# Layer 1 of a two-layer graph network: three product slices folded on GpSimd, thirteen summed on TensorE, extras and additions interleaved

## The reference, cut to what matters

```
R = relu(abs_distances[:, None] @ w1 + b1) @ w2 + b2      # 384 radial weights per edge
Y = spherical_harmonics(rel_vec)
Fj = features[src]                                         # 8 scalars, 8 vectors of 3
for each output block i (lo), input block j (li), lf:
    acc = acc + _NORM[i] * einsum('euv,ef,evi,ofi->euo', Rb[..., k], Yf, Fb, C)
out = zeros.at[dst].add(msg)
x = layernorm(x + out)
```

## Time and profile before

| | us |
|---|---|
| median of 3 runs (lowest to highest) | 1683.98 (1680.54 to 1688.54) |
| the profiled execution's own time | 1679.48 |
| its span | 1677.5 |
| TensorE busy (matmul) | 1287.4, 77% |
| VectorE busy | 1219.6, 73% |
| GpSimd busy | 1007.6, 60% |
| ScalarE busy | 837.2, 50% |
| mean granted TensorE clock | 0.855 |

### The profile page before, as it was taken

One profiled execution on the slowest core, in us unless ns is written; L12 is line 12 of the kernel. 1 busy time (PEld: TensorE's weight loads), 2 busy tenths in 40 slices (PEclk: granted clock), 3 DMA queues, 4 the chain that ended last, 5 costly groups with the idle time before them and its releaser, 6 DMA issues.

```text
span 1677.5 us, 26088 instructions
## 1 busy us (share of the span) xinstructions
PE 1287.4 (77%) x6396; PEld 930.4 (55%) x6396; DVE 1219.6 (73%) x3753; ACT 837.2 (50%) x2256; POOL 1007.6 (60%) x1084
## 2 busy tenths in 40 slices
PE   5699994686413777665677999975999999995773
PEld 1388883243212555555565666653777777775663
DVE  9699996677622343576667999983888888883776
ACT  0167771011101222566675777763665666554984
POOL 7777778777777777776111344446888666600444
PEclk8699997586755999988888999996999999997655
DMA  1100001223224889666455566631232223213785
GB/s 39 23 14 14 15 14 23 51 68 77 69 66 120 250 244 252 173 173 172 119 136 137 172 181 190 184 106 45 61 75 63 59 59 70 65 40 84 204 216 154
DMA packets 310023, 179.32 MB, mean 107 GB/s; under 512 B 29294, under 2 KB 303346, under 8 KB 309874
## 3 DMA queue, kind: packets, MB, share of 16 engines
q1 hardware_dynamic: 231234, 116.84, 26.7%
q0 software_dynamic: 29008, 36.18, 8.6%
q10 hardware_dynamic: 49632, 24.65, 5.1%
HBM read 111.48 MB, written 66.07 MB: 106 GB/s over the span
## 4 chain that ended last, share of the span: by engine, by line
PE 39%; POOL 25%; issue 15%; DMA 10%; DVE 6%; DVEq 2%; ACT 2%; SPq 1%; POOLq 0%; ACTq 0%
PE bank L1042 13%; POOL gat L536 12%; PE bank L1008 7%; POOL lined L544 7%; DMA lined<-in_x,other_i 5%; DVE res L1351 4%; PE bank L1035 3%; DMA placed<-pay,pos_i 3%; PE bank L959 3%; PE bank L1051 3%; POOL out L603 3%; PE bank L1001 3%; PE bank L1017 3%; PE bank L961 2%; POOL placed L555 2%
## 5 line engine op out<-in xcount | busy, mean ns | idle before, releaser
L593 POOL DMA_INDIRECT gat<-x_d,src_i x196 | 238.2, 1215 | 94.8 <-issue 55.7
L1351 DVE TENSOR_TENSOR res<-res,bank 128x128 f32 x588 | 168.5, 287 | 107.2 <-issue 22.6
L536 POOL DMA_INDIRECT gat<-in_x,key_i x196 | 207.0, 1056 | 61.9 <-issue 55.5
L555 POOL DMA_INDIRECT placed<-pay,pos_i x196 | 191.6, 978 | 69.8 <-issue 53.9
L544 POOL DMA_INDIRECT lined<-in_x,other_i x196 | 196.1, 1000 | 59.9 <-issue 48.6
L1042 PE MATMUL bank<-prod,ident 128*128 128x280 f32 x896 | 219.8, 404 | 0.0
L1042 PEld LDWEIGHTS bank<-prod,ident 128*128 128x128 f32 x896 | 168.7, 191 | 54.1 <-issue 15.2
L970 PE MATMUL bank<-woh,pw 128*128 128x128 f32 x784 | 133.4, 332 | 71.4 <-DVE woh L1330 35.8
L970 PEld LDWEIGHTS bank<-woh,pw 128*128 128x128 f32 x784 | 118.5, 235 | 86.7 <-DVE woh L1330 46.2
L56 ACT ACTIVATE xt<-bank 128x128 f32<-128x128 f32 x98 | 26.6, 271 | 264.8 <-PE bank L910 256.2
L890 PE MATMUL bank<-tile_oh,sel 128*128 128x196 f32 x784 | 142.6, 336 | 2.9 <-ACT tile_oh L663 2.0
(11 more groups left out here) (221 smaller groups left out, 2886.2 us busy)
## 6 DMA issues: line engine op xcount, KB each, us to landing
pw<-placed SPq DMA_DIRECT2D x588, 68.0 KB, 2.1
pw<-placed SPq DMA_DIRECT2D x98, 272.0 KB
xin<-in_x_t SPq DMA_DIRECT2D x53, 256.0 KB
placed<-pay SPq DMA_DIRECT2D x49, 272.0 KB, 2.4
x_d<-res POOLq DMA_DIRECT2D x49, 256.0 KB, 3.8
placed<-pay SPq DMA_DIRECT2D x28, 448.0 KB, 3.2
out<-out ACTq DMA_DIRECT2D x49, 256.0 KB, 2.7
xin<-in_x_t ACTq DMA_DIRECT2D x45, 256.0 KB
```

The source lines that it names most:

```text
L536: pool.indirect_dma_start(gat[:, t, :], None, x, bass.IndirectOffsetOnAxis(ap=key_i[:, 0, t:t + 1], axis=0)).then_inc(s_gat[t % G], 16)
L555: pool.indirect_dma_start(placed[1].rearrange("t p r -> (t p) r"), bass.IndirectOffsetOnAxis(ap=pos_i[:, 1, t:t + 1], axis=0), pay[i % 4][ ...
L593: pool.indirect_dma_start(gat1[g % 3][:, k, :], None, x1_d, bass.IndirectOffsetOnAxis(ap=src_i[:, t:t + 1], axis=0)).then_inc(c_gat[g % 3] ...
L1351: add.up(dve.tensor_tensor(into, into, quarter(bank + k // G, k % G), ALU.add))
```

## The change

GpSimd's program gets a second kind of work: `fold_3(g)` adds slices 3 to 5 of `prod[g % 2]` onto slices 0 to 2, in place, when VectorE has written them. It is put behind `gather_3(g + 3)`. TensorE sums slices 6 to 15 first, then waits for the fold (`c_fold`), then sums slices 0 to 2: 13 matmuls. The extras now come one round later, between the second and the third pair of radial steps. On VectorE message and additions are one function: the register read comes first, then the wait for the extras, then message operations and additions in turn (four additions between message operations, three behind the payload). The arithmetic differs only in the order of additions.

```diff
@@ gpsimd
-            for g in range(NU):
-                gather_3(g)
+            def fold_3(g):
+                pool.wait_ge(c_prod, g + 1)
+                some = prod[g % 2][:, :, 0:FOLD, :].rearrange("p t v u -> p t (v u)")
+                more = prod[g % 2][:, :, FOLD:2 * FOLD, :].rearrange("p t v u -> p t (v u)")
+                pool.tensor_tensor(some, some, more, ALU.add).then_inc(c_fold, 1)
+
+            for g in range(NU + 3):
+                if g < NU:
+                    gather_3(g)
+                if g >= 3:
+                    fold_3(g - 3)
@@ tensor
-            def radial(g):
+            def radial(g, lo, hi):
                 pe.wait_ge(c_ht, g + 1)
-                for k in range(0, U, 2):
+                for k in range(lo, hi, 2):
...
-                for v in range(16):
+                for v in [*range(2 * FOLD, 16), *range(FOLD)]:
+                    if v == 0:
+                        pe.wait_ge(c_fold, g + 1)
...
-            radial(0)
-            for g in range(NU + 1):
+            radial(0, 0, U)
+            for g in range(NU + 2):
                 if g + 1 < NU:
-                    radial(g + 1)
+                    radial(g + 1, 0, PAIRED)
+                if g >= 2:
+                    extras(g - 2)
+                if g + 1 < NU:
+                    radial(g + 1, PAIRED, U)
                 if g < NU:
                     sums(g)
-                if g:
-                    extras(g - 1)
@@ vector
+            def message_and_extras_3(g):
+
+                h, behind = g % 2, 0 <= g - 1 < NU
+                to = windows_at(U * (g - 1), U, 1) if behind else None
+                if behind:
+                    dve.wait_ge(c_mm, g)
+
+                def extra(k):
+                    if behind:
+                        add_tile(5, k, to)
+
+                if g < NU:
+                    along = rec[:, U * g:U * g + U, 3:6].unsqueeze(2).broadcast_to([P, U, 8, 3])
+                    dve.wait_ge(c_scal, g + 1)
+                    chain.up(dve.tensor_tensor(rq[:, :, :, :], rest[:, :, 0:8].unsqueeze(3).broadcast_to([P, U, 8, 3]), along, ALU.mult))
+                extra(0)
...
+                extra(3)
+                if g < NU:
+                    dve.wait_ge(c_msg, g + 1)
+                    wait(dve, c_pst[h], 16 * (g // 2))
+                    wait(dve, c_mm, g - 1)
+                    dve.tensor_tensor(pay1[h][:, :, :].rearrange("p t (j f) -> p t j f", j=J),
...
+                for k in range(4, U):
+                    extra(k)
@@
-                if 1 <= g <= NU:
-                    message_3(g - 1)
-                if g >= 2:
-                    extras_3(g - 2)
+                if g:
+                    message_and_extras_3(g - 1)
```

More of the change, by code:

```diff
@@ L300, in gnn_kernel @@
         c_prod, c_sum, c_scal, c_pay, c_mm, c_msg = sem("c_prod"), sem("c_sum"), sem("c_scal"), sem("c_pay"), sem("c_mm"), sem("c_msg")
+        c_fold = sem("c_fold")
         z_pw, z_kr, z_away, z_oh, z_mm = ring(sem, "z_pw", 6), sem("z_kr"), sem("z_away"), sem("z_oh"), sem("z_mm")
@@ L428, in gnn_kernel @@
         RADIAL = (0, 1, 2, 7)
+        PAIRED = 4
+        FOLD = 3
         block = ctx.enter_context(nc.Block())
@@ L1040, in sums @@
                 wait(pe, c_scal, g - 1)
-                for v in range(16):
+                for v in [*range(2 * FOLD, 16), *range(FOLD)]:
+                    if v == 0:
+                        pe.wait_ge(c_fold, g + 1)
                     ins = pe.matmul(psum[3 + g % 2][:, 0:40 * U].rearrange("p (t u) -> p t u", t=U), ident[:, :], prod[g % 2][:, :, v, :],
-                                    start=v == 0, stop=v == 15)
+                                    start=v == 2 * FOLD, stop=v == FOLD - 1)
                 ins.then_inc(c_sum, 1)
@@ L1341, in _, with windows_at @@
             add = Count(s_add)
-            def add_tiles(bank, t0, n, c):
+            def windows_at(t0, n, c):
                 _, to = nc.values_load_multi_w_load_instructions(
@@ L1347, in add_tiles, with add_tile @@
                     skip_runtime_bounds_check_because=IN_RANGE)
+                return to
+            def add_tile(bank, k, to):
+                into = res[:, bass.ds(to[k], 1), :].rearrange("p o c -> p (o c)")
+                wait(dve, add.sem, add.n)
+                add.up(dve.tensor_tensor(into, into, quarter(bank + k // G, k % G), ALU.add))
+            def add_tiles(bank, t0, n, c):
+                to = windows_at(t0, n, c)
                 for k in range(n):
-                    into = res[:, bass.ds(to[k], 1), :].rearrange("p o c -> p (o c)")
-                    wait(dve, add.sem, add.n)
-                    add.up(dve.tensor_tensor(into, into, quarter(bank + k // G, k % G), ALU.add))
+                    add_tile(bank, k, to)
             def add_extra(i, c):
@@ L1454, in products_3 @@
                 ins.then_inc(c_prod, 1)
[L1456 to L1474, removed]
@@ L1476, in extras_3 @@
-            def extras_3(g):
-                dve.wait_ge(c_mm, g + 1)
-                add_tiles(5, U * g, U, 1)
+            def message_and_extras_3(g):
[12 more added lines that the diff above has]
+                if g < NU:
+                    done(chain)
+                    chain.up(dve.tensor_tensor(msg[:, :, 8:32].rearrange("p t (u i) -> p t u i", i=3), rq[:, :, :, :],
+                                               rest[:, :, 8:32].rearrange("p t (i u) -> p t u i", i=3), ALU.add))
+                extra(1)
+                if g < NU:
+                    done(chain)
+                    chain.up(dve.tensor_reduce(mean[:, :], msg[:, :, :], AX_X, ALU.add))
+                extra(2)
+                if g < NU:
+                    done(chain)
+                    dve.scalar_tensor_tensor(out=msgc[:, :, :], in0=mean[:, :].unsqueeze(2).broadcast_to([P, U, D]), scalar=-1.0 / D,
+                                             in1=msg[:, :, :], op0=ALU.mult, op1=ALU.add).then_inc(c_msg, 1)
+                extra(3)
+                if g < NU:
+                    dve.wait_ge(c_msg, g + 1)
+                    wait(dve, c_pst[h], 16 * (g // 2))
+                    wait(dve, c_mm, g - 1)
+                    dve.tensor_tensor(pay1[h][:, :, :].rearrange("p t (j f) -> p t j f", j=J),
+                                      msgc[:, :, :].unsqueeze(2).broadcast_to([P, U, J, D]),
+                                      jm[:, U * g:U * g + U, :].unsqueeze(3).broadcast_to([P, U, J, D]), ALU.mult).then_inc(c_pay, 1)
+                for k in range(4, U):
+                    extra(k)
```

## The result

| | before | after |
|---|---|---|
| median of the runs, us | 1682.6 (4 runs, 1680.5 to 1688.5) | 1702.1 (4 runs, 1693.5 to 1707.0) |
| ratio | | 1.0097 [1.0055, 1.0138] |
| the profiled execution: time (span), us | 1679.5 (1677.5) | 1693.5 (1691.6) |

The changed kernel is slower: the ratio gives 1.0%, and the two medians lie 19.5 us apart. (The four runs of before include the profiled one; their median is therefore not the 1684.0 of the prediction.) The profiled execution of the changed kernel is its shortest run, 14.1 us longer in span than that of before.

The account below looks back on a forecast made before the run. Took TensorE as the bound before and GpSimd's queue after: start +7.9, rounds +16.6, last three -1, tail -0.8, together +22.7 us on 1679.5, 1702.2; on the median 1706.7, stated as 1706, range 1674 to 1724.

Parts of the forecast that it names:

- the rounds: Layer 1 from sums(0) to sums(24): GpSimd sets 13.6 us a round, 24 x 13.6 = 326.4 against 309.8, +16.6 us.
- the start: Layer 1 up to the end of sums(0): the last three terms wait for gather(3) and the first fold, +7.9 us.
- the last three: Layer 1 rounds after sums(24), without gathers: VectorE sets them, about 34 us against 35.0, -1 us.
- TensorE's part: TensorE's round in Layer 1: three sum terms go, 1.45 us; round 10.6 to 11.5 us, taken as 11.4.
- The extras between radial pairs: TensorE's round: extras (1.56 us) fill waits for ScalarE's evictions inside the radial pairs; bounds nothing and 0.9 us.
- VectorE's part: VectorE's round with messages and additions alternated and an uncovered register read of 1.8 us: 11.9 us if nothing else happens.
- The fold: GpSimd's addition of 840 elements per partition: 2.0 us, during which a VectorE operation with two SBUF inputs stands still.
- Losses shrink: Rival: GpSimd's round locks so one gather meets products, 12.45 to 13.0 us; at 12.7, 1685 us; chance 0.17.
- the forecast (13.1 to 14.2): Main case: GpSimd's round in Layer 1 is 13.1 to 14.2 us, time 1694 to 1721 us; chance 0.57.
- the rival in which both engines pay: VectorE loses 2.0 us at each fold and waits for registers; round 14.2 to 14.5, 1723 us; chance 0.12.
- The tail: End of Layer 1 after the last sums: 6.1 us for the last extras and alternated run against 6.9, -0.8 us.
- the marks for the right side: Signs: folds about 2.0 us, sums(0) ending near 1180, sums 13.6 apart, TensorE waiting for GpSimd ahead of the last terms.

Follow-up runs that it names:

- experiment 1: The changed kernel without the fold: TensorE sums sixteen terms again, new order of extras, messages and additions kept; 1679.0 us, 0.9986 against the kernel before.
- experiment 5: The changed kernel with each fold replaced by a GpSimd memset of 1340 elements into an unread tile; 1663.8 us, 0.987 against the kernel before.
- experiment 2: The kernel before with the fold alone, 13 sums and no other part of the change; 1692.9 us, 1.009 against the kernel before.
- experiment 6: The changed kernel with fold(g) behind gather(g+2) and not gather(g+3); 1688.7 us, 1.0048 against the kernel before.
- experiment 3: The changed kernel with the window register read moved from ahead of the message to behind the first product; 1704.7 us, 1.0177 against the kernel before.
- experiment 4: The changed kernel with five gathers a group, not seven, from the fourth group on; 1683.0 us, 1.0031 against the kernel before.

## Why the prediction was right, and where its steps were not

The forecast, GpSimd's queue as the new bound and a slower kernel, came true: predicted 1706, range 1674 to 1724, measured 1702.1. The terms, on the profiled execution (predicted +22.7, measured +14.1), came out less well than the total, and that the total is so near is in part luck: the rounds were put 13.2 us too high, the start and the last three together 6.3 too low, and the unprofiled runs lie above the profiled one for a reason that stays open.

**TensorE's part: right, and worth nothing.** Three terms less is 1.4 us (7.81 to 6.40), and TensorE's own round is below the others'. The extras between radial pairs, which I bounded by 0 and 0.9 and gave 0.1, gave 0.02 in experiment 1.

**VectorE's part: right, 0.4 too long.** I had 11.9 without a block. Its round with a fill in the fold's place is 11.53, and the changed kernel's round less the block is 13.12 - 1.61 = 11.51. The register read costs 1.62 from fk to rq where I took 1.8, the alternated starts are 0.20 to 0.26 apart where I counted 0.21 to 0.31, and the run from rq to products is 3.95 (in experiment 5, where nothing stretches msgc) instead of 4.1.

**The fold: right.** 1.98 us against 2.0. That it stretches a VectorE operation with two SBUF inputs to its own length was right too, from one row: msgc 2.01, rq 1.99, kp 2.09.

**The start: right in kind, 7.9 for 10.0.** The last three terms took 3.17 and not 1.45, which is 1.7 of the 2.1 missing. The table of windows has those 3.17 us (length, busy us of PE, PEld, DVE, ACT, POOL, granted clock):

```profile
1177.29:1180.46 3.17, 3.17 (x8) 1.92 (x10) 0.00 (x0) 0.00 (x0) 2.45 (x3) 0.50 0.05 9
```

The clock is 0.50, the lower of the two levels (1.2 GHz of 2.4), behind 8.85 us in which TensorE did nothing. Of all terms this one has the firmest proof: experiment 2 has it without the new order (+10.2), experiment 6 takes it away by moving the fold.

**The rounds: the step that was mis-sized.** "I take 13.6" is 13.10, and "24 x 13.6 = 326.4: +16.6" measured +3.4. My losses for the gathers added products (1.75 + 0.76) and pay (0.46). Measured are 1.64 + 0.75 + 0.10 - 0.12: the fold, in the rhythm in which the two engines settle, ends just ahead of pay, and the gather behind it starts 0.22 us before pay (1267.84 against 1268.06) and takes 0.96, where before the change a gather that started 0.52 behind pay (1266.82 against 1266.30) took 1.40. The place was an accident of lengths. Where VectorE was relieved (experiment 3) the rhythm broke and the 13.7 appeared, 13.76. So the sum fits a GpSimd that meets everything, and the changed kernel happened to avoid one of the three meetings; I had held the rival "Losses shrink" (12.45 to 13.0) to be only a matter of the products. The 13.10 lies at the very edge between that rival and the forecast (13.1 to 14.2). And I compared GpSimd's 13.6 with a VectorE of 11.9, without its block; with it VectorE has 13.12 and is as full, and experiment 4 shows how near it is: with GpSimd relieved, VectorE sets 13.13 in the mean.

**The last three: wrong in sign.** I had -1, for VectorE at 11.9 without gathers. They are +3.2: a fold that waits for products and not for gathers starts with the features, and blocks the second operation behind the products. GpSimd and VectorE in the first such round:

```profile
1497.85 1.98 POOL L604 TENSOR_TENSOR prod<-prod 128x840 f32<-128x840 f32 x1 [7.54 <-DVE prod L1476]
...
1497.93 2.09 DVE L1461 TENSOR_TENSOR kp<-feat,rec 128x168 f32<-128x168 f32 x1
```

Experiment 4 made the rounds like that one and got 13.27 (three in four). I had priced this block for the rival in which both engines pay and left it out of the term where it was certain.

**The tail: right.** -0.6 against -0.8.

**What would have shown it wrong** did not appear: no GpSimd wait for products in the rounds with gathers, no gathers of 0.94 throughout, no round under 12.6 from sums(3) to sums(24) (from sums(1) to sums(2) it was 11.53, before the rhythm had settled). Of the marks for the right side, one failed: TensorE's wait ahead of the last three terms is there in the first rounds (8.85, 2.37) and gone from sums(3) on, where the fold is done before TensorE comes to it; there the lack shows as TensorE's wait of 1.3 for an eviction, and as VectorE's products in the chain. A bound on GpSimd need not show as a wait for GpSimd when it slows the engine that feeds the one watched.

## What to carry to other kernels

Work given to an engine with "spare" time costs three things besides its own length: what its place in that engine's queue delays at the start of the stage (10 us here), what it takes from the engine that it blocks (1.6 us a round), and what that one takes from it (2.4 to 3.0 a round, the gathers beside products; before the change spare time paid for it). Work these out for each size of the edit, and not for the largest: one slice in place of three, one group earlier, turned +1.0% into -0.9% by moving the bound only as far as the next engine. When two engines block each other, relieving one of them can give nothing, as in experiments 3 and 4, and the round depends on which instructions happen to meet.

## What the runs showed of the hardware that I had not expected

- Relieving VectorE of its register read made rounds longer (13.10 to 13.76), as another pattern took over in which folds fall into products; relieving GpSimd of 2.5 us a round left them as long as they were (13.10 to 13.13).
- A VectorE operation on 224 elements that began 0.25 us ahead of an addition on GpSimd was held to that addition's end: 2.48 us instead of 0.38.
- A fill on GpSimd (1340 elements, 1.24 us) beside a VectorE product leaves it at 2.02 us; an addition there (840 elements, 1.98 us) makes it 3.73.
- The additions on GpSimd took 0.786, 1.386 and 1.978 us for 280, 560 and 840 elements per partition: 0.19 + 0.00213 an element.
- After 8.85 us of waiting six records of a sum took 3.17 us at a granted clock of 0.50; after waits of 0.52 they took 1.68 at 1.00, the same records. The wait just ahead doesn't settle it: in experiment 3, after waits of 2.39 each, they took 3.17 at 0.51 (at 1228.24) and 1.68 at 1.00 (at 1255.64).
